# Attention outputs in 32-column lanes with sums of probabilities, plain row maxima, and a last group scaled in halves

## The reference

```python
Q, K, V = proj(Wq, bq), proj(Wk, bk), proj(Wv, bv)      # 16 heads of 32
Q = Q * cos + rotate_half(Q) * sin; K = K * cos + rotate_half(K) * sin
scores = where(causal, Q @ K^T / sqrt(32), -inf)
out = softmax(scores) @ V                                # 1024 x 1024 for each of 2 x 16 heads
attention = out @ Wo.T + bo
g = (x @ gate_w.T) * gate_s; u = (x @ up_w.T) * up_s     # 512 -> 1408, weights in {-1, 0, 1}
ffn = ((silu(g) * u) @ down_w.T) * down_s
```

## Time and profile before

| | |
|---|---|
| median of 3 executions | 753.57 us (751.13 to 759.17) |
| the profiled execution | 756.7 us, its span 754.9 us |
| PE busy | 732.0 us, 97% |
| DVE, ACT, POOL busy | 442.2, 308.7, 246.4 us |
| PE's share of the chain that ended last | 83% |
| mean granted clock of PE | 0.995 of 2.4 GHz |

### The profile page before, as it was taken

How to read it: one execution, slowest core, us unless ns; L and a number is a source line. 1 busy time by engine, 2 the same in 40 slices (tenths; PEclk the granted TensorE clock), 3 DMA queues, 4 the chain that set the end, 5 groups by cost and what they waited for, 6 DMA issues and landing times.

```text
span 754.9 us, 10665 instructions
## 1 busy us (share of the span) xinstructions
PE 732.0 (97%) x3563; PEld 537.5 (71%) x3563; DVE 442.2 (59%) x1103; ACT 308.7 (41%) x641; POOL 246.4 (33%) x224
## 2 busy tenths in 40 slices
PE   7999999979999999999999999999999999999996
PEld 7788888755665655555555547878788888888884
DVE  6979584987777777777777637863243125114113
ACT  3232232256666666666655562223322232222221
POOL 0626251502114142414141436832232223223222
PEclk9999999999999999999999999999999999999998
DMA  8586568635566666666676475650001001001001
GB/s 281 187 280 232 197 251 278 251 127 158 167 168 180 166 177 181 170 180 175 167 194 167 111 208 171 250 227 1 0 3 55 0 1 56 0 0 56 1 1 58
DMA packets 54318, 104.39 MB, mean 138 GB/s; under 512 B 14820, under 2 KB 18404, under 8 KB 53748
## 3 DMA queue, kind: packets, MB, share of 16 engines
q1 hardware_dynamic: 54264, 103.72, 44.7%
HBM read 69.62 MB, written 38.21 MB: 143 GB/s over the span
## 4 chain that ended last, share of the span: by engine, by line
PE 83%; issue 5%; DVE 4%; DMA 3%; ACT 2%; POOL 2%; SPq 0%; DVEq 0%; POOLq 0%; ACTq 0%
PE ps L1101 38%; PE ps L1240 17%; PE ps L1316 9%; PE ps L1219 8%; PE ps L1126 8%; DMA q_st<-neg_max_T 2%; PE ps L1093 2%; POOL hid_lo L592 1%; ACT p L680 1%; ACT o_raw L687 1%; PE ps L1137 1%; PE ps L1160 1%; SPq L421 0%; DMA x_st<-in_x 0%; DVE stats L796 0%
## 5 line engine op out<-in xcount | busy, mean ns | idle before, releaser
L680 ACT ACTIVATE p<-ps 128x384 f32<-128x384 f32 (+3 forms) x384 | 159.5, 489 | 35.0 <-PE ps L1219 34.4
L841 DVE CUSTOM_DVE_ANT_0 masked<-ps,mask_qk 128x512 bf16<-128x512 f32 (+1 forms) x240 | 113.6, 502 | 66.9 <-PE ps L1126 66.0
L1219 PE MATMUL ps<-q_st,k_st 99*128 99x384 f32 (+2 forms) x384 | 135.6, 361 | 4.2 <-ACT p L680 1.3
L1240 PE MATMUL ps<-p,v_slot 128*64 128x512 f32 (+3 forms) x768 | 137.3, 494 | 0.2 <-ACT o_raw L687 0.2
L1052 DVE SCALAR_TENSOR_TENSOR hid<-ps,us_sb,silu 128x512 f32<-128x512 f32 x44 | 33.0, 751 | 165.2 <-PE ps L1101 159.5
L1126 PE MATMUL ps<-k_st,q_st 96*128 96x512 f32 (+2 forms) x384 | 127.8, 355 | 1.0 <-DVE row_max L841 0.9
L592 POOL TENSOR_TENSOR hid_lo<-hid,hid_hi 128x512 fp32r<-128x512 f32 x44 | 56.8, 1292 | 172.2 <-ACT hid_hi L756 172.2
L561 POOL TENSOR_SCALAR_AFFINE_SELECT p<-p 128x512 f32<-128x512 f32 x64 | 40.7, 637 | 202.9 <-ACT p L680 202.8
L1240 PEld LDWEIGHTS ps<-p,v_slot 128*64 128x64 f32 x768 | 50.1, 136 | 74.3 <-issue 62.0
L1126 PEld LDWEIGHTS ps<-k_st,q_st 96*128 96x128 f32 x384 | 72.5, 190 | 26.4 <-issue 17.7
L1219 PEld LDWEIGHTS ps<-q_st,k_st 99*128 99x128 f32 x384 | 72.3, 190 | 18.7 <-ACT p L680 9.6
(11 more groups left out here) (119 smaller groups left out, 1081.9 us busy)
## 6 DMA issues: line engine op xcount, KB each, us to landing
qk_scratch<-st_hi SPq DMA_DIRECT2D x32, 512.0 KB, 3.8
q_st<-qk_scratch SPq DMA_DIRECT2D x32, 384.0 KB, 3.9
k_st<-qk_scratch SPq DMA_DIRECT2D x32, 384.0 KB, 5.0
flag_st<-in_ffn SPq DMA_DIRECT2D x32, 264.0 KB, 2.8
ffn_copy<-in_ffn SPq DMA_DIRECT2D x32, 264.0 KB, 3.2
qk_scratch<-st_lo SPq DMA_DIRECT2D x16, 512.0 KB, 3.8
o_T<-o_raw SPq DMA_DIRECT2D x32, 128.0 KB, 4.6
rec_l<-rec_rows SPq DMA_DIRECT2D x32, 128.0 KB, 3.3
```

The source lines that it names most:

```text
L680: act.activation(p32[:, at:at + q0 + w - keep], ps[:, ST_BANK + i % ST_RING, keep - q0:w], ACT.Exp, scale=SCALE).then_inc(exp_done, 1)
L841: ins = dve.tensor_tensor_reduce((masked_a if u < 2 else masked)[:, s_before(i) % 2, col:col + kept], scores, mask_qk[:, 512 - kept:512], ...
L1219: pe.matmul(ps[:, ST_BANK + i % ST_RING, 0:w], k_st[0:K_ALL, slot, kt * P:(kt + 1) * P], q_st[0:K_ALL, slot, q0:q0 + w], start=True, stop= ...
L1240: ins = pe.matmul(ps[VW * a:VW * (a + 1), o_bank(u, half), q0 - 512 * half:512], v_slot[:, slot, kt, :], p32[:, at:at + n], start=(kt == 0 ...
```

## The change

- The second half of the queries is handled in two quarters of 256 (`PARTS = 3`, `QW`). For each head the lane of rows 0 to 31 takes V times p (`v`); the lane of rows 32 to 63 takes the sums of p (`l`) and, in other columns of the same bank, V times p of the last key tiles (`w`). So a bank has four lanes of 32 columns of the array. The sum over key tiles 0 to 3 uses p_sum, which POOL adds up with three additions (`sum_p`). The last pair keeps joint products of 64 columns (`PV_TAIL`), with three banks.
- ACT evacuates three times a pair. SP moves six pieces a pair, among them the `w` part to o_w, which `scale_group` adds first (the join). The last pair needs four moves, and they go ahead of bo and ds.
- DVE gives plain maxima (`whole_max`); PE transposes 8 columns ahead of the group of piece 3; ACT negates them to the high part after its third exp; DVE makes the low part (`max_low`).
- The weight test is in two halves at piece 4. Wo is loaded in step 30 over k_st. rec goes to o_T[:, 7], for the last group to rec_last. The last group is scaled in halves of the tokens.

```diff
-M_AFTER = 3
+M_AFTER = 2
-PV_GROUPS = [[(0, 0), (0, 1), (0, 2), (0, 3)], [(1, 0), (1, 1)], [(1, 2), (1, 3), (1, 7)], [(1, 4), (1, 5), (1, 6)]]
+PV_GROUPS = [
+    (0, [[("vl", 0)], [("vl", 1)], [("vl", 2)], [("vl", 3)]]),
+    (1, [[("v", 0), ("w", 4)], [("v", 1), ("l", None)], [("v", 2), ("l", 4)], [("v", 3), ("l", 5)], [("w", 5)]]),
+    (2, [[("v", 0), ("w", 6)], [("v", 1), ("l", None)], [("v", 2), ("l", 4)]]),
+    (2, [[("v", 3), ("l", 5)], [("v", 4), ("l", 6)], [("v", 5), ("l", 7)], [("w", 7)]]),
+]
+PV_TAIL = [
+    PV_GROUPS[0],
+    (1, [[("vl", kt)] for kt in range(6)]),
+    (2, [[("vl", kt)] for kt in range(4)]),
+    (2, [[("vl", kt)] for kt in range(4, 8)]),
+]
...
             def move_pair(u):
-                sp.wait_ge(o_evac, 2 * u + 2)
+                sp.wait_ge(o_evac, PARTS * (u + 1))
...
+                if u == PAIRS - 2:
+                    sp.wait_ge(o_scaled, GROUPS - 1)
...
+                    sp.dma_start(o_w[t // 4 % 2][rows, :], o_raw[l_rows, u % 2, S:S + 2 * QW]).then_inc(o_moved[u % 2], 16)
...
             def b_step(t):
+                if t == HEADS - 2:
+                    sp.wait_ge(st_ps, NPC * t)
+                    sp.dma_start(wo_st[:, :, :], wo).then_inc(wo_in, 16)
...
-            sp.wait_ge(pv_half[1], PAIRS)
+            sp.wait_ge(pv_part[2], part_done(2, PAIRS))
+            move_last_pair()
             sp.dma_start(bo_sb[:, :], bo.partition_broadcast(P)).then_inc(c_in, 16)
             sp.dma_start(ds_sb[:, :], ds.partition_broadcast(P)).then_inc(c_in, 16)
-            move_pair(PAIRS - 1)
...
             def scale_group(g):
                 pool.wait_ge(rec_in, 64 * (g + 1))
-                pool.tensor_tensor(o_T[:, g, :], o_T[:, g, :], rec_l[:, :], ALU.mult).then_inc(o_scaled, 1)
+                pool.tensor_tensor(o_T[:, g, S // 2:S], o_T[:, g, S // 2:S], o_w[g % 2][:, :], ALU.add).then_inc(o_joined, 1)
+                pool.wait_ge(o_joined, g + 1)
+                pool.tensor_tensor(o_T[:, g, :], o_T[:, g, :], rec_of(g), ALU.mult).then_inc(o_scaled, 1)
...
+            def scale_last_group():
+                g, half = GROUPS - 1, S // 2
+                pool.wait_ge(rec_in, 64 * (g + 1))
+                pool.tensor_tensor(o_T[:, g, 0:half], o_T[:, g, 0:half], rec_of(g)[:, 0:half], ALU.mult).then_inc(o_scaled, 1)
+                pool.tensor_tensor(o_T[0:2 * D, g, half:S], o_T[0:2 * D, g, half:S], o_w[g % 2][0:2 * D, :], ALU.add).then_inc(o_joined, 1)
...
+            def sum_p(t):
+                def second_half(kt):
+                    at = t % SLOTS * P_SIZE + P_OFF[kt] + S // 2 - P * kt
+                    return p32[:, at:at + S // 2]
+                total = p_sum[:, t % SUM_SLOTS, :]
+                if t >= SUM_SLOTS:
+                    pool.wait_ge(p_sum_read, 2 * ((t - SUM_SLOTS) // 2 + 1))
+                pool.tensor_tensor(total, second_half(0), second_half(1), ALU.add).then_inc(p_sum_step, 1)
...
             for t in range(HEADS):
                 copy_v(t)
                 if t % 4 == 0 and t >= 8:
                     scale_group((t - 8) // 4)
-                mask_p(t)
+                mask_low(t)
+                if t < HEADS - 2:
+                    sum_p(t)
+                mask_high(t)
...
+                    if t % 2 == 0 and t >= 2 and i == PV_AFTER[0][1]:
+                        evacuate((t - 2) // 2, 1)
...
+            def max_high(u):
+                act.wait_ge(max_T_ps, u + 1)
+                act.activation(neg_hi_T[:, u % 2, :], ps[0:KT, M_BANK, 0:P], ACT.Copy, scale=-1.0).then_inc(max_hi, 1)
...
+            def max_low(u):
+                dve.wait_ge(max_hi, u + 1)
+                dve.scalar_tensor_tensor(out=neg_lo_T[:, u % 2, :], in0=ps[0:KT, M_BANK, 0:P], scalar=-1.0,
+                                         in1=neg_hi_T[:, u % 2, :].bitcast(F32), op0=ALU.mult, op1=ALU.subtract).then_inc(max_T, 1)
...
             def output_products(u, group):
...
-                elif group == PV_HIGH:
+                elif group == 1:
+                    if u < PAIRS - 1:
+                        pe.wait_ge(p_summed, 2 * u + 2)
                     pe.wait_ge(p_high_masked, 2 * u + 2)
...
+                for products in rounds:
                     for a in range(2):
+                        for kind, kt in products:
+                            output_product(u, a, part, kind, kt)
...
                 for i in range(NPC):
-                    if i == M_ENTRY and t < HEADS - 1:
-                        transpose_max(t + 1)
-                    elif i != M_ENTRY and t + 2 < HEADS:
+                    if i != M_ENTRY and t + 2 < HEADS:
                         score_bank(t + 2, i)
                     if t < HEADS:
                         shifted_piece(t, i)
+                    if i == M_ENTRY - 1 and t < HEADS - 1:
+                        transpose_max(t + 1)
```

More of the change, by code:

```diff
@@ L159, in transformer_block @@
             xst_c = sb("xst_c", [P, TJ, H], F32, after_wo)
-        wo_st = sb("wo_st", [P, KC, H], F32)
+        p_sum = sb("p_sum", [P, SUM_SLOTS, S // 2], F32)
+        o_w = [sb(f"o_w{k}", [P, S // 2], F32) for k in range(2)]
         with ExitStack() as after_v:
@@ L273, in transformer_block @@
         p_high_masked = sem("p_high_masked")
-        pv_half = [sem(f"pv_half{k}") for k in range(2)]
+        p_sum_step = sem("p_sum_step")
+        p_summed = sem("p_summed")
+        p_sum_read = sem("p_sum_read")
+        pv_part = [sem(f"pv_part{k}") for k in range(PARTS)]
         o_evac = sem("o_evac")
```

222 lines of the change are left out of this document (138 added, 84 removed).

## The result

The changed kernel takes 761.75 us (median of 20 executions, 754.68 to 768.34) where the kernel before takes 755.2 (20 executions, 751.13 to 759.17). The ratio, which leaves out four executions of the changed kernel that were over 1.5% above its fastest, is 1.008, 95% interval 1.006 to 1.010: 6 us slower. The forecast was 741, range 733 to 754. The profiled execution took 760.33 us, span 758.6, against 756.7 and 754.9 before.

What follows compares the result with a forecast made beforehand. PE bounds the kernel (97% busy, full clock), so streamed columns and short waits count. Terms -17.6, -0.6, -1.1, +4.5, +2.0 sum to -12.8 us: 756.7 to 743.9, or 741 on the median's scale; range 733 to 754.

Steps and rivals of the forecast that it cites:

- Output groups and evacuation: Fourteen head pairs of attention: shorter output groups save 1.07 us a pair, transpose and copy off the chain 0.19; -17.6 us.
- the first of my two formulas: Groups 1 to 3: lanes go on by themselves, 2560 columns, 4.76 us with starts; the other, rounds wait for longest, 5.19.
- both lane rivals: Groups 1 to 3: fewer lanes at once, about 792 us, chance 0.13; four lanes hindering each other, about 749, chance 0.12.
- the figure of the Trainium skill for three tiles: Three column tiles 2.38 times faster, 0.79 of full per tile; four as 3.17 would save 0.2 us a pair.
- the middle that I took: Groups 1 to 3: saving of 1.07 us a pair, between 1.29 and 0.86.
- DMA and max rows: Six scaling steps: 128 KB more ahead of the max rows, 0.75 us more each, +4.5 us (bounds 0 and 9).
- Maxima: zero: DVE in attention: operations dropped and gained stay within 0.2 us of 6.8 a step; zero, bound +0.3 a pair.
- Sums of key tiles: zero: Three POOL additions a head, 3.9 us, still under PE; zero with 1.9 us to spare, bound +1.5 in six steps.
- Start, -1.1: Start of attention: PE's first transpose needs DVE's first small operation, not its last; -1.1 us (0 to -1.2).
- Pairs 14 and 15: Steps 30 and 31: shorter groups bring perhaps half, -0.6 us (0 to -1.3); last pair and Wo load zero.
- Behind the last pair: After attention: last moves ahead of bo and ds, plus a join, delay next chunk's bias adds; +2.0 us (0 to 3.5).
- the gain comes and waits eat it: Rival: late max rows in all even steps, ACT 0.57 us behind, or late POOL sums; 746 to 753, near 748; chance 0.17.

Runs made afterwards that it cites:

- the joined kernel: Changed kernel with space behind xT 192 bytes longer, max rows before moves where t % 4 == 0, bo/ds before last moves, chunk 1 bias adds between last-group halves: 747.34 us, 0.9916.

## Why the prediction was wrong, step by step

The lanes brought what was forecast, and the rest of the sum failed: 741 forecast, 761.75 measured, 21 us apart on the medians (trace against trace 743.9 and 760.3, 16.4 apart, of which the changed trace has 3.0 us of luck ahead of its first product on xT). The terms one by one, forecast first:

- **Output groups and evacuation, -17.6: right.** Plain pairs lose 1.38 us against 1.26. The lanes go on by themselves: 1024 columns x 4 / 2400 + 0.165 = 1.87, 768 columns 1.44, the first of my two formulas. Four run at once at full pace, against both lane rivals and the figure of the Trainium skill for three tiles, quoted in the prediction. The three groups give 1.31 of it, more than the middle that I took. The transposes and ACT's third copy together give 0.07, where I had 0.19 and zero. Fourteen pairs: -19.3.
- **DMA and max rows, +4.5: the step that failed most.** The six scaling pairs lose 14.0 us against a plain pair, where all pairs of before lost 1.8 (258.4 less 14 x 18.33): +12.2, of which 3.4 are half clock by estimate. I wrote that SP's six issues end when the max rows are due. In the pair shown they end 2 us behind DVE's negation; the max rows are issued 3.5 us behind the start of the first output group, where before it was 2.9 (304.96 against 302.06), and take 5.0 to land instead of 4.3. I priced bytes, and left out the two issues' place in the queue and the clock. The run with the max rows first in these steps gives 6.5 us back.
- **"Maxima: zero", DVE within 0.2 us of 6.8 a step: failed.** In the pairs DVE has 204.0 us, 7.3 a step, for a step that became shorter. I took two half tests for one whole: with POOL idle they are 2 x 0.43 against 0.70, and with POOL's sums 2 x 0.60 in the mean of all. The runs that took either away show 6.0 and 6.6 us behind it, which overlap with the line above.
- **"Sums of key tiles: zero": right for POOL** (no wait of PE for p_sum), wrong for what POOL does to DVE.
- **Start, -1.1: failed, +4.0.** That the first shifted piece comes 2.5 us sooner is the 3.0 us of luck. Counted from the first product on xT it comes 0.5 later (110.42 against 109.91), since the distance between operands costs 1.1 in stage A. The first group starts 16.5 us behind it instead of 14.5, and takes 1.5 longer. The half clock from 168.9 on is 3.4 of these 3.5 us by estimate. DVE's full windows don't make it by themselves: the joined kernel's profiled execution has them as full and has PE's wait of 1.0 us too, but no half clock, and there the first group starts 14.8 us behind. What made the clock fall is open. Its windows:

```profile
154.69:162.69 8.00, 7.93 (x35) 5.36 (x33) 8.00 (x33) 6.63 (x16) 3.10 (x3) 1.00 0.26 72
162.69:169.50 6.81, 5.75 (x26) 3.83 (x25) 6.78 (x25) 5.17 (x13) 6.58 (x8) 1.00 0.74 210
```

- **Pairs 14 and 15, -0.6: right within its bounds**, -1.3 (14.62 us against 15.88).
- **Behind the last pair, +2.0 (up to 3.5): failed.** +6.4. I had the bias adds 2.4 us later; they begin 4.2 later, counted from the last pair's first group. SP holds bo and ds not only behind the last four moves, but those behind pair 14's six, which begin at 446.72, when POOL has multiplied group 6. The last group takes 8.0 us instead of 5.6, where I had 1.3 more: the join of 64 rows took 1.82. The half clock at 476.1 adds 1.7 by estimate.
- **Missing: the feed-forward stage, +4.3** (1.3 in each of two chunks, less in the outer two). The space behind xT became 192 bytes shorter, and no step of mine asked what moves with it.
- **Missing: the clock.** No term priced a fall of it. Its 8.5 us lie inside the lines above.

The differences between measured and forecast, scaling steps 7.7, groups -1.7, start 5.1, pair 14 -0.7, tail 4.4 and feed-forward stage 4.3, give 19.1; less the 3.0 of luck that is 16.1 of the 16.4. The rival "the gain comes and waits eat it" named the late max rows; its late sums and ACT's copies did not come. It reached 748, 753 at most: right in kind, and short by the clock, the tail and the layout.

## What to carry to other kernels

A queue's order is a chain: before adding an issue, an operation or a wait, list what stands behind it, through to the matmul; here two added DMAs cost more by place than by bytes. Ask what PE's clock does to a plan with new waits: here stretches at half clock made some 8.5 us of a trace, and their number differs between executions of one kernel. Price two engines that read SBUF side by side not by their rows alone. After any change to a buffer's length, compare a stage that was not edited, matmul start to start, since it may tell of the layout. And before reading a small difference between two traces, find out what differs ahead of the part that was edited.

## What was not expected of the hardware

- Four column lanes of 32, float32, unequal streams, run fully beside one another: 24 records in 1.43 us.
- The distance between the weights and the streaming operand of a 128 x 512 matmul sets its pace: 227 ns at the three multiples of 256 bytes tried, 233 in the mean 64 and 128 bytes over. That was 4.3 to 4.6 us in the feed-forward stage, 1.1 to 1.3 in stage A, and 7 in the ratios.
- A half test of DVE held up by an addition of POOL ends 0.29 to 0.30 us behind that addition, in all seven cases of the changed kernel.
- The length of a wait does not tell whether the clock falls. In the changed kernel PE's matmuls waited 1.2 and 1.9 us (until 342.0 and 379.9) and 3.4 us at half clock followed; 0.9 and 1.1 us (until 233.5 and 269.3) were not followed by any. But in the joined kernel a wait of 1.65 us (until 340.8) wasn't either, and the same wait of 1.0 us at the start was followed by 6.8 us at half clock in the one trace and by none in the other. What decides isn't shown.
